# First attention's V and the low-rank slot projection from split float32r operands, slot scores as one stacked float32r pass

## The reference

```
x = x + attention_a(layernorm(x))     # 16 heads of 128, causal softmax
x = x + ffn(layernorm(x))             # per-token int8 quantisation, 256 x 256
x = x + attention_b(layernorm(x))     # gated slot attention, 16 heads, 64 slots
x = x + ffn(layernorm(x))
```

## Time and profile before

| | |
|---|---|
| median of three executions | 920.13 us |
| executions | 923.7, 920.13, 918.7 us |
| the profiled execution, first to last instruction | 922.5 us |
| TensorE matmul, busy | 817.4 us (89%) |
| VectorE, busy | 683.4 us (74%) |
| ScalarE, busy | 482.6 us (52%) |
| GpSimd, busy | 292.7 us (32%) |
| first attention's loop, 34.6 to 310 us | TensorE busy 275.4 of 275.4 us |

### The profile page before, as it was taken

The page is one execution under the profiler, slowest core; times in us unless marked ns, Lnnn a source line. Parts: engine busy times, 40 slices in busy tenths (PEclk is TensorE's granted clock), DMA queues, the critical chain, the costliest instruction groups (busy, mean ns, idle before and its releaser), DMA issues.

```text
span 922.5 us, 14194 instructions
## 1 busy us (share of the span) xinstructions
PE 817.4 (89%) x4428; PEld 687.2 (74%) x4428; DVE 683.4 (74%) x1500; ACT 482.6 (52%) x1280; POOL 292.7 (32%) x287
## 2 busy tenths in 40 slices
PE   3999999999999846998998998998989989989963
PEld 2788888888888734876887787787778768767852
DVE  6455545454545688698889889888888988987876
ACT  3455555465455325565574664755656655555420
POOL 7011011010010145244344353362452553442222
PEclk9999999999999979998999999998999999989997
DMA  7011010110110010001001001001000010000001
GB/s 223 1 46 40 5 45 0 45 45 0 45 63 5 1 58 1 1 12 47 0 11 45 0 11 45 11 0 46 11 27 18 11 45 0 11 0 0 1 1 45
DMA packets 23653, 23.74 MB, mean 26 GB/s; under 512 B 2369, under 2 KB 23361, under 8 KB 23506
## 3 DMA queue, kind: packets, MB, share of 16 engines
q1 hardware_dynamic: 23634, 23.51, 8.1%
HBM read 22.45 MB, written 1.05 MB: 25 GB/s over the span
## 4 chain that ended last, share of the span: by engine, by line
PE 61%; POOL 12%; issue 10%; DVE 9%; ACT 6%; DMA 1%; POOLq 0%; ACTq 0%; SPq 0%; DVEq 0%
PE ps L1202 12%; PE ps L1396 9%; PE ps L1207 6%; PE ps L1230 4%; PE ps L1309 4%; POOL rot_s L417 4%; PE ps L1457 4%; PE ps L1273 3%; ACT wv L710 2%; PE ps L1249 2%; DVE xn L777 2%; POOL wc_lo L358 2%; DVE qp L1018 2%; PE ps L1314 2%; POOL qp L436 2%
## 5 line engine op out<-in xcount | busy, mean ns | idle before, releaser
L358 POOL TENSOR_TENSOR w_lo<-w_raw,w_hi 128x512 fp32r<-128x512 f32 x32 | 43.7, 1378 | 218.0 <-ACT w_hi L501 218.0
L1202 PE MATMUL ps<-xT_hi,w_hi 128*128 128x512 f32 x256 | 110.0, 430 | 3.1 <-DVE xT_lo L784 1.9
L1202 PE MATMUL ps<-xT_hi,w_lo 128*128 128x512 f32 x256 | 101.5, 397 | 0.0
L417 POOL TENSOR_TENSOR rot_s<-rot_s,const 128x512 f32<-128x512 f32 x64 | 89.4, 1408 | 38.0 <-ACT rot_s L637 38.0
L1202 PE MATMUL ps<-xT_lo,w_hi 128*128 128x512 f32 x256 | 100.9, 394 | 0.0
L957 DVE TENSOR_TENSOR rot<-rot,const 128x512 f32<-128x512 f32 x64 | 74.1, 1158 | 28.7 <-ACT rot_s L637 28.7
L987 DVE TENSOR_TENSOR wt<-ps,const 128x384 f32<-128x384 f32 x128 | 68.2, 550 | 10.8 <-PE ps L1458 8.1
L545 ACT ACTIVATE wt<-wt,negmax 128x128 f32<-128x128 f32 (+1 forms) x128 | 56.6, 444 | 36.1 <-DVE negmax L853 36.1
L841 DVE TENSOR_TENSOR v<-ps,bv_b 128x256 f32<-128x256 f32 x64 | 26.9, 422 | 59.5 <-PE ps L1207 59.4
L1207 PE MATMUL ps<-wv,xT 128*128 128x256 f32 x256 | 63.1, 380 | 1.0 <-DVE v L841 1.0
L1396 PE MATMUL ps<-wc_hi,xT_hi 128*128 128x512 f32 x128 | 60.6, 473 | 1.3 <-ACT rot_s L637 0.7
(11 more groups left out here) (158 smaller groups left out, 2327.8 us busy)
## 6 DMA issues: line engine op xcount, KB each, us to landing
w_raw<-a_w_q SPq DMA_DIRECT2D x8, 256.0 KB, 3.4
w_raw<-a_w_k SPq DMA_DIRECT2D x8, 256.0 KB, 3.8
wv<-a_w_v SPq DMA_DIRECT2D x8, 256.0 KB, 2.5
wo<-a_w_o SPq DMA_DIRECT2D x8, 256.0 KB, 3.3
w_raw<-b_Wq SPq DMA_DIRECT2D x8, 256.0 KB, 2.6
w_raw<-b_Wk SPq DMA_DIRECT2D x8, 256.0 KB, 3.4
wc<-b_Wv SPq DMA_DIRECT2D x8, 256.0 KB, 3.5
wc<-b_Wg SPq DMA_DIRECT2D x8, 256.0 KB, 3.9
```

What stands on the lines that cost most here:

```text
L358: g.tensor_tensor(lo[:, :, :], raw[:, :, :], hi[:, :, :].bitcast(F32), ALU.subtract).then_inc(ph.w_lo, 1)
L417: g.tensor_tensor(ap, ap, const[:, col:col + T].unsqueeze(1).to_broadcast([P, 2, T]), ALU.mult).then_inc(b_rotmul, 1)
L1202: ins = mm(PJ[n[0]], w[:, m, c, h * P:(h + 1) * P], x[:, c, cols], start=(t == 0), stop=(t == len(terms) - 1))
```

## The change

Four edits.

1. V of the first attention: `wv` is split like the other weights (ScalarE `wv_hi`, GpSimd `wv_lo`), and a V tile becomes six float32r products of 256 columns (`proj_v`). The split is a third one per pair: ScalarE's in step b = 2 ahead of the exponentials, GpSimd's last in its body. In the prologue ScalarE's comes after the copy of q1, and GpSimd's between the second `split_tail` and the memsets. The DMA of `wv` follows those of q and k under one wait.
2. `xT` is gone, and with it one of the two ScalarE copies of every transposed half.
3. `s1_product` becomes six float32r products of 256 columns whose 96 weight columns hold the rank three times at a distance of 32. ScalarE adds a constant column (`s1b`, the ones at rows 16 and 80) and rounds (`s1_hi`), and then VectorE overwrites rows 32 to 47 with the rest (`s1_tail`).
4. The slot scores take these 96 stacked rows against a stacked `ws2s`, in one float32r product per tile of 128 tokens. TensorE waits for VectorE's `s1_tail` where it waited for ScalarE's copy.

```diff
-            sp.wait_ge(init_done, 5)
-            sp.dma_start(ws2[0:RANK, :], b_ws2).then_inc(small_ld, 16)
-            sp.dma_start(ws2[BIAS_ROW:BIAS_ROW + 1, :], ...).then_inc(small_ld, 16)
+            sp.wait_ge(init_done, 2)
+            for q in range(3):
+                sp.dma_start(ws2[q * QUAD:q * QUAD + RANK, :], b_ws2).then_inc(small_ld, 16)
+            for q in (0, 2):
+                bias_row = q * QUAD + RANK
+                sp.dma_start(ws2[bias_row:bias_row + 1, :], ...).then_inc(small_ld, 16)
                 sp.wait_ge(a.w_lo, a.splits * i)          # a.splits: 2 before, 3 after
                 load_qk(a, a_wq, a_wk, cols)
-
-                sp.wait_ge(a.proj_ps, 2 * NA * i)
                 load_v(cols)
# GpSimd
             split_tail(a, 0, 1)
+            split_tail(a, 0, 2)
             def zero_outputs():
...
+            pool.wait_ge(ws1_hi_done, 1)
+            dup = ws1[:, :, :].unsqueeze(2).to_broadcast([P, C, 3, RANK])
+            g.tensor_tensor(ws1_lo[:, :, :, 0:RANK], dup, ws1_hi[:, :, :, 0:RANK].bitcast(F32), ALU.subtract
+                            ).then_inc(ws1_done, 1)
             with pool.Fori(0, PAIRS - 1) as i:
                 split_tail(a, i + 1, 0)
                 split_tail(a, i + 1, 1)
                 split_out_tail(a, i, wo)
+                split_tail(a, i + 1, 2)
# ScalarE
-                s.activation(xT[:, :, cols], src, ACT.Copy)
                 s.activation(xT_hi[:, :, cols], src, ACT.Copy).then_inc(xts[m].hi, 1)
...
-                s.activation(s1[0:RANK, ...], ps[0:RANK, ...], ACT.Copy).then_inc(s1_done, 1)
+                s.activation(s1s[0:STACK, ...], ps[0:STACK, ...], ACT.Identity,
+                             bias=s1b[0:STACK, :]).then_inc(s1_hi, 1)
...
+                    if b == 2 and not last:
+                        act.wait_ge(a.proj_ps, 2 * NA * i + 2 * NA)
+                        split_head(a, i + 1, 2)
...
                 if f == 0:
                     transposed(0, 2, 4)
                     transposed(0, 3, 5)
+                if f == 1:
+                    split_head(a, 0, 2)
             a_exp_step(0)
-            act.wait_ge(small_ld, 16 * 7)
+            act.wait_ge(small_ld, 16 * 10)
+            act.wait_ge(init_done, 5)
+            s.activation(ws1_hi[...], ws1[...] three times, ACT.Copy).then_inc(ws1_hi_done, 1)
+            s.activation(ws2s[0:STACK, :], ws2[0:STACK, :], ACT.Copy).then_inc(ws2_hi_done, 1)
# VectorE
-            d.memset(s1[BIAS_ROW:BIAS_ROW + 1, :], 1.0).then_inc(ones_done, 1)
+            d.tensor_tensor(s1b[:, :], const[...], const[...], ALU.add).then_inc(ones_done, 1)
+            def s1_tail(b):
+                dve.wait_ge(s1_hi, b + 1)
+                low, cols = slice(QUAD, QUAD + RANK), slice(b * T, (b + 1) * T)
+                d.tensor_tensor(s1s[low, cols], ps[low, ffns[0].banks[b], 0:T], s1s[low, cols].bitcast(F32),
+                                ALU.subtract).then_inc(s1_done, 1)
...
+            dve.wait_ge(ws2_hi_done, 1)
+            low = slice(2 * QUAD, 3 * QUAD)
+            d.tensor_tensor(ws2s[low, :], ws2[low, :], ws2s[low, :].bitcast(F32), ALU.subtract).then_inc(ws2_done, 1)
             with dve.Fori(0, PAIRS - 1) as i:             # first attention's loop
...
             tail(1, 1, ffns[0].banks[1])
+            s1_tail(0)
+            s1_tail(1)
             ln_scale(1, 3)
             ffn_quant(0, 3)
...
             b_gate(n0(8), 0, 2, 0)
+            s1_tail(2)
             b_okn_max(0, 0, 0)
             b_slots(0)
             b_recip(None, 0, 2)
+            s1_tail(3)
             with dve.Fori(0, PAIRS - 1) as i:             # second attention's loop
# TensorE
             def s1_product(b):
                 pe.wait_ge(xts[1].lo, b + 1)
-                for c in range(C):
-                    ins = mm(ps[0:RANK, ...], ws1[:, c, :], xT[:, c, b * T:(b + 1) * T], ...)
+                terms = [(c, w, x) for c in range(C) for w, x in ((ws1_hi, xT_hi), (ws1_hi, xT_lo), (ws1_lo, xT_hi))]
+                for t, (c, w, x) in enumerate(terms):
+                    ins = mm(ps[0:STACK, ...], w[:, c, :, :].rearrange("p q r -> p (q r)"),
+                             x[:, c, b * T:(b + 1) * T], ...)
                 ins.then_inc(s1_ps, 1)
-            def proj_tile(bank_ap, w, tile):
-                for c in range(C):
-                    ins = mm(bank_ap, xT[:, c, tile * P:(tile + 1) * P], w[:, c, :], ...)
+            def proj_v(bank_ap, tile):
+                cols = slice(tile * P, (tile + 1) * P)
+                terms = [(c, x, w) for c in range(C) for x, w in ((xT_hi, wv_hi), (xT_hi, wv_lo), (xT_lo, wv_hi))]
+                for t, (c, x, w) in enumerate(terms):
+                    ins = mm(bank_ap, x[:, c, cols], w[:, c, :], ...)
                 return ins
                     if name == "v0":
-                        pe.wait_ge(a.wv_ld, pair * 16 + 16)
+                        pe.wait_ge(a.w_lo, pair * a.splits + 3)
...
+            pe.wait_ge(ws1_done, 1)
             s1_product(0)
             s1_product(1)
             ffn_transpose(0, 2)
             pe.wait_ge(s1_done, 2)
-            pe.wait_ge(ones_done, 1)
+            pe.wait_ge(ws2_done, 1)
...
-                        ins = mm(PJ[bank][...], s1[:, tile * P:(tile + 1) * P], ws2[:, bass.ds(pair * P, P)], ...)
+                        ins = mm(PJ[bank][...], s1s[0:STACK, tile * P:(tile + 1) * P],
+                                 ws2s[0:STACK, bass.ds(pair * P, P)], ...)
```

More of the change, by code:

```diff
@@ L49 @@
 RANK = 16
-BIAS_ROW = 32
+QUAD = 32
+STACK = 3 * QUAD
 SCALE = float(P) ** -0.5
@@ L102, in layer_kernel @@
         wv = sb("wv", [P, C, 2 * P])
+        wv_hi = sb("wv_hi", [P, C, 2 * P], F32R)
+        wv_lo = sb("wv_lo", [P, C, 2 * P], F32R)
         wc = sb("wc", [P, C, 4 * P])
@@ L133, in layer_kernel @@
         ws1 = sb("ws1", [P, C, RANK])
-        s1 = sb("s1", [P, B * T])
-        ws2 = sb("ws2", [P, HEADS * M])
+        ws1_hi = sb("ws1_hi", [P, C, 3, 32], F32R)
+        ws1_lo = sb("ws1_lo", [P, C, 3, 32], F32R)
+        s1b = sb("s1b", [P, 1])
+        s1s = sb("s1s", [P, B * T], F32R)
+        ws2s = sb("ws2s", [P, HEADS * M], F32R)
         rot = sb("rot", [P, 2, HALF])
@@ L143, in layer_kernel @@
         esT = sb("esT", [P, B * T])
+        ws2 = esT[:, :]
         enz = sb("enz", [P, TILES, 2 * M])
@@ L356, in split_tail @@
                 pool.wait_ge(ph.w_hi, ph.splits * n + m + 1)
-                raw, hi, lo = (wc, wc_hi, wc_lo) if m == 2 else (w[:, m, :, :] for w in (w_raw, w_hi, w_lo))
+                value = {"a_": (wv, wv_hi, wv_lo), "b_": (wc, wc_hi, wc_lo)}[ph.name]
+                raw, hi, lo = value if m == 2 else (w[:, m, :, :] for w in (w_raw, w_hi, w_lo))
                 g.tensor_tensor(lo[:, :, :], raw[:, :, :], hi[:, :, :].bitcast(F32), ALU.subtract).then_inc(ph.w_lo, 1)
@@ L497, in split_head @@
             def split_head(ph, n, m):
-                act.wait_ge(ph.wv_ld if m == 2 else ph.wqk_ld, n * 32 + 32)
-                raw, hi = (wc[:, :, :], wc_hi[:, :, :]) if m == 2 else (w_raw[:, m, :, :], w_hi[:, m, :, :])
+                if m < 2:
+                    act.wait_ge(ph.wqk_ld, n * 32 + 32)
+                    raw, hi = w_raw[:, m, :, :], w_hi[:, m, :, :]
+                elif ph is a:
+                    act.wait_ge(a.wv_ld, n * 16 + 16)
+                    raw, hi = wv[:, :, :], wv_hi[:, :, :]
+                else:
+                    act.wait_ge(b_.wv_ld, n * 32 + 32)
+                    raw, hi = wc[:, :, :], wc_hi[:, :, :]
                 s.activation(hi, raw, ACT.Copy).then_inc(ph.w_hi, 1)
@@ L1182, in s1_product @@
                 pe.wait_ge(xts[1].lo, b + 1)
-                for c in range(C):
-                    ins = mm(ps[0:RANK, ffns[0].banks[b], 0:T], ws1[:, c, :], xT[:, c, b * T:(b + 1) * T],
-                             start=(c == 0), stop=(c == C - 1))
+                terms = [(c, w, x) for c in range(C) for w, x in ((ws1_hi, xT_hi), (ws1_hi, xT_lo), (ws1_lo, xT_hi))]
+                for t, (c, w, x) in enumerate(terms):
+                    ins = mm(ps[0:STACK, ffns[0].banks[b], 0:T], w[:, c, :, :].rearrange("p q r -> p (q r)"),
+                             x[:, c, b * T:(b + 1) * T], start=(t == 0), stop=(t == len(terms) - 1))
                 ins.then_inc(s1_ps, 1)
@@ L1203, in proj_qk @@
                 ins.then_inc(ph.proj_ps, 1)
[L1205 to L1207 removed]
+            def proj_v(bank_ap, tile):
+                cols = slice(tile * P, (tile + 1) * P)
+                terms = [(c, x, w) for c in range(C) for x, w in ((xT_hi, wv_hi), (xT_hi, wv_lo), (xT_lo, wv_hi))]
+                for t, (c, x, w) in enumerate(terms):
+                    ins = mm(bank_ap, x[:, c, cols], w[:, c, :], start=(t == 0), stop=(t == len(terms) - 1))
                 return ins
@@ L1365, in b_task @@
                         tile = HT * half + t
-                        ins = mm(PJ[bank][:, t * P:(t + 1) * P], s1[:, tile * P:(tile + 1) * P],
```

(3 more changed lines are left out.)

32 lines of the change are left out of this document (20 added, 12 removed).

## The result

The changed kernel takes 927.39 us (median of nine executions, 925.66 to 929.0), the kernel before 923.7 beside it (nine, 918.7 to 924.81). The medians differ by 3.7 us. The ratio on record, which isn't the quotient of the two medians, is 1.0055 [1.0039, 1.0072], or 5.1 us [3.6, 6.7]: the change made the kernel about half a per cent slower. Of the kernel before's 88 executions on record 23 lie at 918.4 to 920.5 us, 63 at 921.4 to 925.5, and two, which no ratio uses, at 1053.79 and 2073.61.

What follows compares the result with a forecast made beforehand. TensorE was taken to bound the first attention's loop, with engine handoffs elsewhere. Start +2.3, loop -5.9, third split 0, between the attentions with the entry +3.4, slot scores 0 gave -0.2: 920.13 to 919.9 us, range 911 to 926.

Steps and rivals of the forecast that it cites:

- V products and the loop: First attention's loop: six products per V tile take 0.72 us; 0.39 saved per odd step, -5.9 us in all.
- the fourth: Rival: the second loop's first body swallows the prologue shifts, 0 for +3.4, giving 916.5 us; chance 12%.
- the second: Rival: V tiles in the first attention's loop pay in full, -8.7 for -5.9, giving 917.1 us; chance 12%.
- third: Rival: weight loads pace narrow products, a V tile takes 1.14 us, giving 942 us; chance 8%.
- The start: Prologue: earlier transposes are given back as GpSimd shuts out VectorE's L862 and TensorE's clock drops: +2.3 us.
- The first rival: Prologue: VectorE's L862 gets in beside GpSimd; start gives -4.1 us, all together 913.5 us; chance 20%.
- Third split, start casts: The loop's extra split of wv and the start's bigger ws1 and ws2 casts fit into idle time: 0 each.
- Between the attentions: VectorE's queue behind the wait for s1_tail(1): normalisation and quantisation come later, the clip 1.2 us late.
- The entry: Second loop's entry: s1_tail(2) delays b_okn_max, and TensorE also waits for s1_tail(3): +2.2 us.
- Slot scores: Second attention: 15 tasks of some 0.9 us shrink by half or more, but TensorE waits for ScalarE's z: 0.
- Bounds of both together (+3.4): Delays between the attentions and at the second loop's entry: +3.4 us, bounds 0 and +5.
- The base: Whole kernel: the sum was put on the median 920.13 us; the profiled span of 922.5 counted as scatter.

Runs made afterwards that it cites:

- e1: Only the V part, on the kernel before; slot projection and slot scores stay float32: 919.08 us, ratio to before 0.9963.
- e2: Only the slot part (projection, stacked scores, VectorE's subtractions), on the kernel before; V stays float32: 931.1 us, ratio to before 1.0091.
- e5: The changed kernel, but between the attentions VectorE normalises the last batch ahead of batch 1's subtraction: 925.86 us, ratio to before 1.0032.
- e4: The changed kernel, but at the start GpSimd's bias addition waits for VectorE's first four normalising multiplications: 921.52 us, ratio to before 0.9976.
- e3: The changed kernel, with VectorE's last two subtractions reordered at the second loop's entry and TensorE's wait moved inside the loop: 921.89 us, ratio to before 0.9992.
- e7: The changed kernel with the new orders of e3, e4 and e5 together: 914.33 us, ratio to the kernel before 0.9906.
- e8: e1 plus e4's start order, so the V part without the slot part: 914.62 us, ratio to the kernel before 0.9904.
- e6: The changed kernel plus unread TensorE products, eight in the last body's pause and eleven at the second loop's entry: 925.77 us, ratio to before 1.0024.
- e11: The kernel before, with GpSimd's wait for all normalised x moved ahead of its five memsets: 919.27 us, ratio to before 0.9963.

## Why the prediction was wrong

The mechanisms were nearly all there. One term of the sum, the handoff between the attentions, came out above even the upper bound that I gave it, and the base that the sum was put on was too low. Each step, forecast against trace:

- **V products and the loop**: -5.9 forecast. An odd step is 0.36 shorter (0.39 forecast), -5.4 in all. Products 0.12 apart, no pacing by weight loads, and the last two tiles pay 0.07 net, as `oT_hi` is waited for. Right. e1 shows that a gain reaches the end and e2 that a loss does, so of the rivals the fourth was wrong, the second and third too. The prediction's 197.27 for the output group's first column doesn't follow from its own rows (197.44 + 0.93 less four times 0.23 is 197.45); nothing hangs on it.
- **The start**: +2.3 forecast, 0.0 to +0.2 in the profiled execution, +2.0 in e5's. The shut-out (L862, now L907) is as forecast: 5.12 us, and the last V tile at 32.17 for 32.75. The 2.9 us for the clock was one execution's value for something that varies: 1.5 in the profiled execution (0.19 x 8), 3.1 in e5's. The first rival (L862 gets in, -4.1) didn't come true; e4 reaches -5.0 by an order of instructions.
- **Third split, start casts**: 0 and 0; no trace contradicts.
- **Between the attentions**: +1.2 forecast, 1.57 at the clip. e5 confirms the place. Then q0's products run cold; up to `kT` another 0.9 is lost.
- **The entry**: +2.2 forecast (its own terms give 2.1), 2.3 measured (the shift goes from -1.5 at `kT` to +0.81 at the transposes). Its parts are as forecast: `ok` 1.6 late for 1.64, 1.04 of it left at `qp` for 1.1, and 1.37 more for the last subtraction. e3 takes all of it away.
- **Slot scores**: 0 forecast; e7 and e8 confirm it.
- **The failed step** is "Bounds of both together (+3.4): 0, if the queues behind catch up, and +5, if idle TensorE drops its clock here". The sum took +3.4. TensorE did drop its clock: behind 3.13 us at the entry (+1.43; e3 and e6 take it away), on q0 (+0.9), and behind the 2.43 us of the last body (+1.25), where the pause was as long before and I had not looked; there it is open whether that is chance alone (e6). The transition costs 7.4, not 3.4; without the last body 6.2, above even the bound of 5.
- **The base** failed too. The sum was put on 920.13, the median of three executions, two of which are among the 23 lowest of the 86: bad luck. The rows, however, came from a slower one. Its span of 922.5 was held against times, as lying within their scatter, but every execution of it on record takes 1.8 to 1.9 us more than its span, so the profiled one took some 924.3. On nine executions' 923.7 the same sum gives 923.5.

By traces the sum is +0.2 - 5.4 + 1.25 + 1.57 + 0.9 + 2.3 + 1.43 = +2.25 where +2.24 was measured at B; forecast was -0.2. From 919.9 to 927.39 it is 7.5 us: 3.6 are the base, 2.2 the difference of the spans against the forecast's -0.2, and 1.6 are that the profiled execution after lies 1.0 under its median and the profiled one before 0.6 over its own. That the ratio says +5.1 and the medians 3.7 I can't place; its interval [3.6, 6.7] takes in both. The range ended at 926 because the slower cases were priced with the clock up, or as one big mechanism at 942; moved up by the 3.6 of the base it would have ended at 929.6 and held the result, with the transition as wrong as before.

## What to carry to other kernels

An edit that shortens the bound loop and puts a small step at a handoff is judged at the handoff: write down what stands behind each new wait on its queue, and what the bound engine does meanwhile, since its pause can cost twice, once as idle time and once as work at half clock. Put a small dependent instruction where its queue already waits, and its consumer's wait at the first use, not ahead of the loop. And look at which elementwise instructions are much longer than their kind elsewhere in the same trace; here one moved wait was worth as much as the arithmetic. And take the base from more than three executions, and from the same kind that the rows come from.

## What the runs showed of the hardware

- VectorE's SBUF-to-SBUF `tensor_scalar` is shut out by GpSimd's instructions: four took 5.12 us beside an add of 4.50 and 0.99 without it (e4); 6.86 beside a split and memsets and 2.42 beside the split alone (e11). The Trainium skill ("SBUF — State Buffer", SBUF: two separate sides) has an exclusive lock held for a whole instruction. The single add agrees with it; the 6.86 us, in which a split and five memsets follow one another without a gap and VectorE isn't let in between two of them, go beyond it. So do the 6.06 us beside a split and three memsets between the attentions.
- TensorE's clock is at its lower level (1.2 GHz, 0.50) behind a pause of 3.13 us every time at the entry (four traces), but in seven of thirteen at the first products behind one of 3.1 us for `kT`, and in five of ten behind one of 2.43 us. At the start it comes back after 3 to 6 us of work, differently in executions of the same instructions (full change and e5).
- Products of 256 columns with new weights for each ran 0.12 us apart, though a weight load is 0.19 long: in the step shown above the loads start 0.12 apart as well (192.67, 192.79, 192.91), so one overlaps the next.
